# One row product in float32r parts, and a vector stage cut out of the routing's block, in a two-layer network on one core

## The reference, cut to what matters

```python
# x: 8 batches of 512 tokens by 256. Layer 0:
h = layernorm(x) * (1 + ca) + sa                  # ca, sa, ga, cb, sb, gb: rows per batch
normed = layernorm(h) * ln_g + ln_b
hid = silu(normed @ W_hidden + b_hidden)          # 256 -> 1024
v, gate = hid[..., :512], hid[..., 512:]          # "value and gate rows"
qk = silu(normed @ W_qk + b_qk)                   # 256 -> 512
q, k = qk * gamma[0] + beta[0], qk * gamma[1] + beta[1]
attn = softmax(einsum('bid,biD->bdD', q, k) / 512)
x = x + ga * ((v * attn.sum(-1) * gate) @ W_out + b_out + h)
f = layernorm(x) * (1 + cb) + sb
shared = (silu(f @ sw1) * (f @ sw3)) @ sw2        # shared expert, 256 -> 512 -> 256
s = sigmoid(f @ router_w.T)                       # 8 experts, the top 2 of each token
routed = sum over the 2 chosen of gate_e * (gelu(f @ ew1[e]) @ ew2[e])
x = x + gb * (shared + routed)
# Layer 1: a selective state space mixer (convolution, 16 states, a scan over 512 tokens),
# then an MLP with four ternary matrices; both with their own layernorm and rows.
```

## Time and profile before

| | |
|---|---|
| three runs | 2625.68 us (median), 2623.66, 2636.82 |
| profiled execution | 2636.68 us, span 2634.9 us |
| mean granted TensorE clock | 0.935 |
| busy, share of the span | PE 87%, PEld 56%, DVE 66%, ACT 51%, POOL 50% |
| the chain that ended last, by engine | PE 51%, DVE 17%, issue 11%, ACT 10%, POOL 4%, DMA 2% |
| instructions | 26906 |

### The profile page before, as it was taken

The page is one execution under the profiler, slowest core; times in us unless marked ns, Lnnn a source line. Parts: engine busy times, 40 slices in busy tenths (PEclk is TensorE's granted clock), DMA queues, the critical chain, the costliest instruction groups (busy, mean ns, idle before and its releaser), DMA issues.

```text
span 2634.9 us, 26906 instructions
## 1 busy us (share of the span) xinstructions
PE 2303.8 (87%) x8452; PEld 1462.8 (56%) x8452; DVE 1735.8 (66%) x2782; ACT 1353.0 (51%) x1793; POOL 1316.8 (50%) x1135
## 2 busy tenths in 40 slices
PE   2799989999898986678998998998998988998978
PEld 1456657566575652235665555555555555565666
DVE  3445454554545449899689689689689689688730
ACT  0233425334253354546766766766766765766622
POOL 1232332522324215556667666666666666667833
PEclk6899999999999997888999998998999998999989
DMA  8034564455444464444555544655554644546622
GB/s 267 0 109 151 162 194 156 141 161 159 155 137 137 126 219 118 129 127 132 171 141 134 172 144 132 170 142 133 170 142 136 174 139 126 170 136 172 192 72 91
DMA packets 253773, 384.77 MB, mean 146 GB/s; under 512 B 19168, under 2 KB 159984, under 8 KB 253632
## 3 DMA queue, kind: packets, MB, share of 16 engines
q1 hardware_dynamic: 223408, 281.33, 36.9%
q0 software_dynamic: 30224, 101.73, 12.5%
HBM read 345.93 MB, written 47.55 MB: 149 GB/s over the span
## 4 chain that ended last, share of the span: by engine, by line
PE 51%; DVE 17%; issue 11%; ACT 10%; POOL 4%; DMA 2%; DVEq 0%; another core or an unknown queue 0%; POOLq 0%; SPq 0%; ACTq 0%
PE bank L235 27%; PE bank L241 7%; PE bank L1494 7%; PE bank L242 7%; DVE bank L1416 4%; DVE w_st L1424 4%; POOL d_in L1406 2%; DVE cv L1236 2%; ACT bank L1472 1%; DMA bc<-bc_rows 1%; ACT L1472 1%; DVE mid L1596 1%; PE bank L1052 1%; POOL f1L L1572 1%; ACT L1645 1%
## 5 line engine op out<-in xcount | busy, mean ns | idle before, releaser
L1406 POOL TENSOR_TENSOR d_in<-u,bc 128x512 f32<-128x512 f32 x512 | 661.8, 1303 | 386.6 <-DMA bc<-bc_rows 300.6
L1416 DVE TENSOR_TENSOR_SCAN bank<-bank,d_in 128x512 f32<-128x512 f32 x512 | 624.9, 1222 | 98.7 <-ACT bank L1472 71.3
L1494 PE MATMUL bank<-w_st,ident 128*128 128x512 f32 x1024 | 540.4, 642 | 93.2 <-DVE w_st L1424 92.9
L1472 ACT ACTIVATE bank<-dt,a_neg 128x512 f32<-128x512 f32 x512 | 348.0, 690 | 463.4 <-DVE w_st L1424 461.6
L1424 DVE TENSOR_TENSOR w_st<-bank,bc 128x512 f32<-128x512 f32 x512 | 345.2, 674 | 120.7 <-PE bank L1494 120.4
L241 PE MATMUL bank<-f1H,w_ring 128*128 128x512 f32 x768 | 361.6, 471 | 60.9 <-ACT raw L1305 22.4
L1494 PEld LDWEIGHTS bank<-w_st,ident 128*128 128x128 f32 x1024 | 197.8, 202 | 310.2 <-DVE w_st L1424 177.2
L242 PE MATMUL bank<-f1L,w_ring 128*128 128x512 f32 x768 | 312.0, 406 | 0.0
L205 POOL TENSOR_TENSOR norm_rstd<-norm_veps,minus_half 128x4 f32<-128x4 f32 x24 | 25.7, 1072 | 423.2 <-DVE norm_veps L201 423.0
L241 PE MATMUL bank<-f0H,w_ring 128*128 128x512 f32 x512 | 228.4, 446 | 3.6 <-POOL f0L L1572 3.6
L1572 POOL TENSOR_TENSOR f0L<-mid,f0H 128x512 fp32r<-128x512 f32 x128 | 170.0, 1329 | 122.7 <-DVE f0H L1600 86.6
(11 more groups left out here) (202 smaller groups left out, 3846.5 us busy)
## 6 DMA issues: line engine op xcount, KB each, us to landing
bc<-bc_rows SPq DMA_DIRECT2D x256, 512.0 KB, 5.0
w_ring<-w_units POOLq DMA_DIRECT2D x160, 512.0 KB, 4.2
w_exp<-L_ffn_ew SPq DMA_DIRECT2D x240, 256.0 KB, 4.6
eo_rows<-eo SPq DMA_DIRECT2D x56, 256.0 KB, 4.5
xs<-xs_rows SPq DMA_DIRECT2D x24, 512.0 KB, 4.0
w_units<-h_T SPq DMA_DIRECT2D x16, 512.0 KB
xA<-L_attn_x SPq DMA_DIRECT2D x8, 512.0 KB, 6.1
x_mid<-xA SPq DMA_DIRECT2D x8, 512.0 KB
```

The source lines that it names most:

```text
L1406: pool.tensor_tensor(d_in[:, nth(b, s) % IN, :], u[:, c, :], rows_tile(b, use)[:, 0, :], ALU.mult).then_inc(in_made.sem, 1)
L1416: dve.tensor_tensor_scan(bank[:, :], bank[:, :], d_in[:, nth(b, s) % IN, :], 0.0, ALU.mult, ALU.add).then_inc(scanned.sem, 1)
L1472: act.activation(state_bank(b, s)[:, :], dt[:, c, :], ACT.Exp, scale=a_neg[:, c, n:n + 1]).then_inc(dA_made.sem, 1)
L1494: pe.matmul(y_bank(c)[:, :], ident[:, :], w_st[:, nth(b, s) % WG, :], start=False, stop=(n == NST - 1)).then_inc(summed.sem, 1)
```

## The change

1. **Hidden product.** `W_hidden` is loaded into what later holds expert weights and split once, at the start, into two float32r parts, `w_hidH` (ACT) and `w_hidL` (POOL). For every batch ACT writes `nT` a second time as float32r, `nTH`, and POOL subtracts to get `nTL`. Each of the 16 float32 products of a batch becomes three float32r products: high by high, low by high, high by low. POOL's addition of `b_out` moves behind the subtractions.
2. **Shared expert.** The four multiplications become a stage of their own (`shared_vector`), whose places 41.6 and 43.6 put the first two between the two series of the routing. PE's down product starts with the inner parts k = 0, 1, 2 of both tiles before it waits for the fourth multiplication; it takes both banks first.
3. **Memory.** `w_dt` and `w_out` of layer 1 no longer stay for the whole program; they are loaded with `w_in` at the start of layer 1's first front, with a semaphore of their own.
4. **Order.** 25 places of the three plans get other values.

```diff
-    fetch=4.5, ... norm_stats=26, ... conv=45.7, raw_gap=11.7, ... h_second=97, ... gate_second=23.1,
-    ... rows_in=3.3, input=2.6, ... out_add=14.5, ... m_act=6.3, ... hid_pe_odd=1.6
+    fetch=4.1, ... norm_stats=25.1, ... conv=45.6, raw_gap=11.8, ... h_second=99.7, ... gate_second=21.4,
+    ... rows_in=3.2, input=2.5, ... out_add=14.2, ... m_act=7.1, ... hid_pe_odd=1.9
 PLAN_A
-    after=72.2, x_in=36, rows_in=49.8, sim_max=15, fT=38.1, r_sig=41, rank=44, eo_out=9.4
+    n_low=-0.1, after=72.0, x_in=31.3, rows_in=48.6, sim_max=14.7, fT=39.4, r_sig=40.9, rank=43.2, eo_out=9.9
 PLAN_LAST
-    rank=40, gather=19.4, slots=41, s2=46, s2_out=46.6, scatter=43
+    rank=37.5, gather=19.7, slots=41.6, s2=46.4, s2_out=48.7, scatter=44.0

 setup_sync
-                sp.dma_start(w_dt[:, :], ins["L1_attn_W_dt"]).then_inc(ssm_weights_in.sem, 16)
-                sp.dma_start(w_out[:, :, :], k_tiles(ins["L1_attn_W_out"])).then_inc(ssm_weights_in.sem, 16)
 setup_pool
+                pool.wait_ge(hid_weights_in.sem, 2 * 16)
+                pool.wait_ge(w_hid_split.sem, 1)
+                pool.tensor_tensor(w_hidL[:, :, :], w_hid, w_hidH[:, :, :].bitcast(F32), ALU.subtract).then_inc(w_hid_split.sem, 1)
 setup_scalar
+                act.wait_ge(hid_weights_in.sem, 2 * 16)
+                act.activation(w_hidH[:, :, :], w_hid, ACT.Copy).then_inc(w_hid_split.sem, 1)

 att_pool
-                yield x1 - 4
+                for k in range(KD):
+                    yield x1 + PLAN_A["n_low"] + k
+                    pool.wait_ge(*nT_made.at(b, KD + k + 1))
+                    pool.tensor_tensor(nTL[:, k, :], nT[:, k, :], nTH[:, k, :].bitcast(F32), ALU.subtract).then_inc(n_low.sem, 1)
+                yield x1 + 4.5
 att_scalar
+                for k in range(KD):
+                    act.activation(nTH[:, k, :], att_bank(b, k)[:, :], ACT.Identity, bias=lnc[:, 1, k:k + 1], scale=lnc[:, 0, k:k + 1]
+                                   ).then_inc(nT_made.sem, 1)
 att_tensor
-                    products(tile(6 + j)[:, :], lambda k: w_hid[:, k, half * HID + d * P:half * HID + (d + 1) * P],
-                             lambda k: nT[:, k, :], KD).then_inc(hid_done.sem, 1)
+                    if j == 0:
+                        pe.wait_ge(*n_low.all(b))
+                    bank, of = tile(6 + j), slice(half * HID + d * P, half * HID + (d + 1) * P)
+                    for k in range(KD):
+                        pe.matmul(bank[:, :], w_hidH[:, k, of], nTH[:, k, :], start=(k == 0), stop=False)
+                        pe.matmul(bank[:, :], w_hidL[:, k, of], nTH[:, k, :], start=False, stop=False)
+                        i = pe.matmul(bank[:, :], w_hidH[:, k, of], nTL[:, k, :], start=False, stop=(k == KD - 1))
+                    i.then_inc(hid_done.sem, 1)

 ffn_vector
+            def shared_vector(b):
                 for m in range(KS):
-                    yield x1 + plan_of(b)["s_mul"] + 2 * m
+                    yield x1_at(b) + plan_of(b)["s_mul"] + 2 * m
                     dve.wait_ge(*s1_act.at(b, m + 1))
                     dve.wait_ge(*s3_done.at(b, m + 1))
 ffn_tensor
+                yield x1 + plan_of(b)["s2"]
+                tiles = [ffn.take(("s2", b, n), s2_out.at(b, n + 1)) for n in range(2)]
+                def down(n, j, k):
+                    t = 2 * n + j
+                    return pe.matmul(tiles[n][:, j * D:(j + 1) * D], s_act[:, k, t * P:(t + 1) * P], w_s2[:, k, :], start=(k == 0),
+                                     stop=(k == KS - 1))
+                for k in range(KS - 1):
+                    pe.wait_ge(*s_made.at(b, k + 1))
+                    for n in range(2):
+                        down(n, 0, k)
+                pe.wait_ge(*s_made.all(b))
                 for n in range(2):
-                    yield x1 + plan_of(b)["s2"] + 2 * n
-                    pe.wait_ge(*s_made.all(b))
-                    token_products(ffn.take(("s2", b, n), s2_out.at(b, n + 1)), n, lambda k: s_act[:, k, :], lambda k: w_s2[:, k, :], KS
-                                   ).then_inc(s2_done.sem, 1)
+                    down(n, 0, KS - 1)
+                for n in range(2):
+                    for k in range(KS):
+                        i = down(n, 1, k)
+                    i.then_inc(s2_done.sem, 1)
 front_sync
+                    sp.dma_start(w_dt[:, :], ins["L1_attn_W_dt"]).then_inc(w_late_in.sem, 16)
+                    sp.dma_start(w_out[:, :, :], k_tiles(ins["L1_attn_W_out"])).then_inc(w_late_in.sem, 16)
```

More of the change, by code:

```diff
@@ L26 @@
 PLAN = dict(
[L27 to L31, removed]
+    fetch=4.1, xB_in=8.8, w3_in=88.0, haste=0.38, rows_out=106.9, norm_rstd=29, norm_stats=25.1, norm_apply=34.2,
@@ L34 @@
[L34 removed]
+    up_low=10.0, hid_low=11.8, m_apply=5, up_gate=6.0, last_add=1.5, m_act=7.1, up_act=2.2, hid_act=8.7, m_turn=4.4,
+    up2_pe=1.9, hid_pe_odd=1.9, last_pe=-1.1)
 PLAN_A = dict(
[L39 to L41 removed]
@@ L42 @@
-    route=41.3, shared=37.1, s1_act=32.1, s_mul=41.6, rank=44, slots=43.8, s2=51.2, s2_out=50.6, scatter=45,
-    xs_in=5, w_list=5, w_first=7.5, w_second=-1.6, xsT=0.3, e_act=1.2, eo_out=9.4, gather=3, combine=8, x_out=10,
-    experts=(6, 10, 12.2, 17, 20, 22.4, 25.5, 28, 33.5, 36))
+    n_low=-0.1, unit=7.0, stretch=1.87, after=72.0, last=55.2, last_gap=2.4, turn=68.2, x_in=31.3, rows_in=48.6,
+    rates=37.1, stats1=27.1, norm1=21.7, stats2=14, norm2=11.2, q_mul=7.1, q_add=9.2, sim=15.3, sim_max=14.7,
@@ L47 @@
+    sim_exp=16.5, gated=23, wo=26.4, wo_add=26.2, f_stats=29.8, f_rstd=36.7, f_norm=34.7, f_turn=38, fT=39.4,
+    router=40, r_sig=40.9, route=41.3, shared=37.1, s1_act=32.1, s_mul=41.6, rank=43.2, slots=43.8, s2=51.2,
+    s2_out=50.6, scatter=45, xs_in=5, w_list=5, w_first=7.5, w_second=-1.6, xsT=0.3, e_act=1.2, eo_out=9.9,
+    gather=3, combine=8, x_out=10, experts=(6, 10, 12.2, 17, 20, 22.4, 25.5, 28, 33.5, 36))
 PLAN_LAST = dict(
     f_stats=31.7, f_rstd=31, f_norm=32, f_turn=34.5, fT=34.8, router=38.5, r_sig=36, route=36.3, shared=36.5,
-    s1_act=36.4, s_mul=37.9, rank=40, e_act=1.7, eo=1.6, eo_out=8.2, gather=19.4, combine=27.3, x_out=29, slots=41,
@@ L50 @@
-    s2=46, s2_out=46.6, scatter=43)
+    s1_act=36.4, s_mul=37.9, rank=37.5, e_act=1.7, eo=1.6, eo_out=8.2, gather=19.7, combine=27.3, x_out=29,
+    slots=41.6, s2=46.4, s2_out=48.7, scatter=44.0)
 class Signal:
@@ L305, in adaln_kernel @@
             nT = sb("nT", [P, KD, S])
+            nTH, nTL = (sb(n, [P, KD, S], F32R) for n in ("nTH", "nTL"))
             qk_tok = sb("qk_tok", [P, 2, TT, HID])
@@ L1094, in adaln_kernel @@
             w_in = sb("w_in", [P, KD, 2 * INTER])
+            w_dt, w_out = sb("w_dt", [DTR, INTER]), sb("w_out", [P, KI, D])
             xB, gaB = sb("xB", [P, TT, D]), sb("gaB", [P, D])
@@ L1338, in dt_tile @@
                 def dt_tile(c):
+                    if b == 0 and c == 0:
+                        pe.wait_ge(*w_late_in.all(0))
                     bank = shared.take(("dt", b, c), relu_made.at(b, c + 1))
```

31 lines of the change are left out of this document (18 added, 13 removed).

## The result

| | before | after |
|---|---|---|
| median (runs) | 2626.17 us (4) | 2598.0 us (4) |
| lowest, highest | 2623.66, 2636.82 | 2597.22, 2603.71 |
| profiled execution, span | 2636.68, 2634.9 us | 2597.4, 2595.7 us |

The ratio is 0.9884, with a 95% interval of 0.9862 to 0.9907: 28 us between the medians. Forecast were 2588 us, 2566 to 2610. Between the two profiled executions the difference is 39.2 us, where the sum of the prediction said 37.9.

The account below looks back on a forecast made before the run. Layer 0 was taken as bound by PE except some 7 us a batch, layer 1 by PE and DVE. 18.2 + 13.2 + 4.7 + 4.0 + 1.8 - 4 = 37.9 us off 2636.7 gives 2599, less 11: 2588 us, range 2566 to 2610.

Parts of the forecast that it names:

- hidden product, 7 batches: Layer 0's hidden product: three float32r products per float32 one shorten PE's time before the similarity, 2.6 us a batch, 18.2 us.
- stretch, 6 middle batches: Layer 0, shared expert to next attention: moved multiplications shorten DVE's chain by 2.2 us in 6 batches, 13.2 us gained.
- first batch's stretch: Layer 0's first batch: POOL's last scatter, not DVE's combination, sets the second xhatA, 157.9 against 162.60, 4.7 us gained.
- last batch: Last batch of layer 0: a 3.46 us wait and 1.9 us of low clock go; 4.0 of 5.4 us taken.
- clock at the new waits: PE in layer 0: a clock fall at qk costs up to 2.1 us; 0.7 us in 6 batches, 4 us lost.
- start, first rows: Kernel start: SP no longer issues w_dt and w_out before the first rows, which come 1.8 us earlier.
- layer 1: Layer 1's moved places only exchange neighbours, worth at most 11 us either way; nothing was booked.
- the keys hold the similarity: Rival, chance 0.11: POOL's k chain moves back, so the hidden product's change gains nothing, costing 20 us: 2606.
- POOL does not extend the chain: Layer 0, before the second xhatA: POOL is free at 595.5 and asked for its reciprocal deviation at 595.9.
- PE gets all it could: Rival, chance 0.06: DVE's combination is out of the way in time, 3.7 us a batch more on top of 2.2: 2566.
- a fall at each new wait: Rival, chance 0.09: PE's clock falls at each new wait, costing 12.6 us instead of 4: 2596.
- that wait hides it: Kernel start: DVE's 20.78 us wait for rows from memory hides the weight split, 5.9 us on POOL.

Follow-up runs that it names:

- e7: Changed kernel with the last two steps of DVE's combination moved behind the next attention's second normalisation: 2612.44 us, 0.9906 of before.
- e12: e8 with POOL's second reciprocal deviation ahead of the last three scatters and DVE's multiplication by the rows CA ahead of the second series: 2563.20 us, 0.9711 of before.
- e8: Changed kernel with e6 and e7 together, POOL's two reciprocal deviations, DVE's first normalisation and two row operations moved earlier: 2586.24 us, 0.9802 of before.
- e6: Changed kernel, but POOL's subtraction for the low part of the hidden weights waits until DVE has made the modulation rows: 2598.05 us, 0.9848 of before.
- e11: Changed kernel with one place of layer 1 as before, DVE's statistics of the next batch behind one more scan: 2612.31 us, 0.9905 of before.
- e1: The kernel before, unchanged, profiled a second time: 2630.81 us, ratio 1.0011.

## Why the prediction was right, and where it was not

The ledger between the two profiled executions, in us:

| step | predicted | measured |
|---|---|---|
| hidden product, 7 batches | -18.2 | 7 x (73.69 - 71.15) = -17.8 |
| stretch, 6 middle batches | -13.2 | 6 x (35.63 - 32.95) = -16.1 |
| first batch's stretch | -4.7 | 35.13 - 37.96 = -2.8 |
| last batch | -4.0 | 19.60 - 24.91 = -5.3 |
| clock at the new waits | +4 | +4.4 |
| start, first rows | -1.8 | 66.55 - 62.98 = +3.6 |
| first attention | 0 | 63.43 - 61.66 = +1.8 |
| layer 1 | 0 | 1710.9 - 1717.8 = -6.9 |
| sum | -37.9 | -39.2 (unrounded) |

The sum came within 1.3 us of the measured 39.2, and that is luck in part: six rows of the ledger are off by more than 1 us, -2.9 (stretch), -1.3 (last batch) and -6.9 (layer 1) one way, +1.9 (first batch's stretch), +5.4 (start) and +1.8 (first attention) the other way, and they nearly cancel.

**Hidden product: right.** 0.233 us a product, 2.54 us a batch, and the slack before the similarity used up, to 0.4 us. The rival in which the keys hold the similarity is refuted.

**Stretch: right in its mechanism.** DVE's chain sets the end, PE waits in front of the down product (2.12 us, forecast 2.7) and for `xhatA` (1.88, forecast 2.2, or 0.19 where the down product runs low). DVE's chain itself, from its second series to the next attention, went from 20.47 to 18.07 us in the mean of six batches, 2.4 a batch for the 2.2 forecast. The rest of the 16.1 us was not in the sum: the second series starts 0.8 us sooner behind the start of the rank counts (1.89 in place of 2.72), and these come 0.6 us later behind the start of the stretch (12.99 in place of 12.43), as PE's first 16 products, before the counts, run low in five of the six batches and did in four. The step said that POOL does not extend the chain, with 0.4 us to spare. In the changed kernel nothing is to spare, and e7 shows what the step overlooked: the next cut on DVE would have met POOL's scatters. "PE gets all it could" needed both, and in e12, which has both, the stretch is 6.5 us shorter than before (35.63 - 29.12), where that rival had 2.2 + 3.7 = 5.9. No row gives its 3.7.

**First batch's stretch: mis-sized.** From the rank counts on it lost 23.41 - 19.18 = 4.2 us, near the 4.7 forecast, with POOL as the last to arrive. Ahead of the counts it gained 1.4 us, as PE's first 16 products took 9.86 us in place of 8.48. The sum had no term for that.

**Clock: right in size, in part by luck.** Of the waits of about 1.9 us for `xhatA` one in four had `qk` at 8.83 us in place of 7.13, 1.7 us; behind the 3.46 us of the first batch it took 9.61, with 2.7 us more for that attention: together 4.4. The term of 4 us was for the six middle batches, which cost 1.7; the first batch's was not in it. The rule that the prediction weighed, from the Trainium skill, "TensorE: Matmul & The Clock Gate", "What's actually happening", says that only activity releases the throttle. The rival drawn from it, a fall at each new wait, did not come true here: three of four such waits passed without one, and over the eight traces that have such waits, this one among them, 22 of 26. It did in e7, where the waits are 3.0 to 4.3 us, at all six. The length of the one wait doesn't decide it alone: in e8, with 1.4 to 2.2 us, `qk` ran slow behind five of six.

**Start: wrong, by 5.4 us.** The failed step is "that wait hides it": DVE's wait for rows does cover the split's own time, but the split runs beside the very work that ends in these rows. I looked at the engine that waits, and not at what it waits for. e6 puts it right and gets 4 us back. The 1.8 us of Part 3 came to about 1.1: from the store of the modulation rows to the first load of rows (`rowsA`) it is 22.33 us in e6, 23.40 before. The first attention is 1.8 us longer on top, which no run here takes apart.

**Layer 1: mis-sized.** "I take nothing" out of 11 us either way; it was -6.9 in the traces and about 10 us by the medians of e11. The price of a swap was put at one DVE pass. The trace of before had the difference in it: the same normalisation took 1.36 us in the one batch where POOL stood idle meanwhile, and 1.83 to 4.32 beside POOL's products in the six later ones. Two of these rows of before, the second with POOL's:

```profile
1012.97 1.36 DVE L210 TENSOR_SCALAR cv<-xB,normB_stat,normB_rstd 128x256 f32<-128x256 f32 x4
...
1580.18 2.79 DVE L210 TENSOR_SCALAR cv<-xB,normB_stat,normB_rstd 128x256 f32<-128x256 f32 x4
...
1579.60 1.29 POOL L1406 TENSOR_TENSOR d_in<-u,bc 128x512 f32<-128x512 f32 x1
1581.39 1.43 POOL L1406 TENSOR_TENSOR d_in<-u,bc 128x512 f32<-128x512 f32 x1 [0.50 <-DMA bc<-bc_rows]
```

A move on DVE can be worth what it then runs beside.

**From trace to median: wrong in part.** The sum fitted the profiled executions, but between the medians it was 28 us in the first comparison, so that 2598 came out 10 us above the forecast 2588, and 36 in the second. To take the whole difference off a median 11 us below the profiled execution assumed that these 11 us had nothing to do with the change; e1 shows that some lie in the stretch that the change shortens. Which share of them is the kernel's and which is chance stays open.

**Readings.** Two readings of the prediction don't hold as they stand. Of the 725 us which the chain of waits lays on line 235, 94 lie in layer 1. And the terms give a beat of 109.1 - 2.6 - 2.2 + 0.7 = 105.0 us for layer 0, not 104.5; measured were 104.8 in the mean.

## What to carry to other kernels

An engine that waits hides new work only if that work leaves alone the chain it waits for: follow the wait back to its source before booking it at nothing. Before an order is changed, list the durations of the same instruction over all batches; where they differ, look at what stood beside the long ones, as that is what the new order can gain or lose. And where two engines arrive within a few tenths, shortening one alone can cost time: move the second engine's link first.

## What was not expected of the hardware

A two-input subtraction on POOL (128x2048, 4.56 us) stretched a DVE multiplication on 8x512 with two inputs from SBUF from 0.68 to 4.86 us, so that it ended 0.5 us behind the subtraction. In e6 the same subtraction ran beside DVE's statistics (BATCH_NORM_STATS2, one input), and these took 1.40 us as before. POOL's products of 1.3 us doubled the four DVE operations of the normalisation, from 1.37 to 2.79 us. The Trainium skill, "GPSIMD Engine Reference", "1. Specifications", says that POOL shares its SBUF interfaces with DVE, with contention for DVE instructions that have two SBUF inputs or run in a 2-port mode; the traces agree for the multiplication, and show besides that the normalisation, with one tensor input, is hit too. For the latter the Trainium skill would need it to run in such a mode, which no run here shows directly. That a one-input TENSOR_SCALAR on 8x512 took 0.41 us at the start and the two-input TENSOR_TENSOR 0.68 would fit.
